# Two attention heads side by side in TensorE's array, slots placed anew, and a third of the pooling on ScalarE

## The reference

```python
# x: (64, 12, 224, 224); channel_weights (12, 192)
pooled = x.reshape(B, 12, 14, 16, 14, 16).sum(axis=(3, 5))       # patches of 16 x 16
h = einsum('bcij,ce->bije', pooled, channel_weights)             # 196 tokens of 192
h = h + attention1(layernorm(h))                                 # one head, Wq, Wk, Wv
x = layernorm(h)
# router: softmax over 4 experts; each expert takes its top 98 of 196 tokens
# expert e sees the first 24, 48, 96 or 192 channels; h1 = xg @ w1.T + b1, summed over experts
x_mlp, x_qkv = h1[..., :768], h1[..., 768:]
attn = softmax(q @ k.T * 16 ** -0.5)                             # 12 heads of 16, 196 x 196
y2 = concat(gelu(x_mlp), attn @ v)
o = (gathered y2 @ w2.T + b2) * mask, weighted by the gate, halves added
out = h + (x + o)
```

## Time and profile before

| | |
|---|---|
| median of 3 runs | 1757.34 us (1749.19 to 1767.99) |
| profiled execution | 1757.22 us, span 1755.4 us |
| mean granted clock of TensorE | 0.939 |
| busy: PE, DVE, ACT, POOL | 1517.8, 1218.5, 847.3, 248.9 us |
| mean DMA rate | 124 GB/s |

### The profile page before, as it was taken

One profiled execution on the slowest core, in us unless ns is written; L12 is line 12 of the kernel. 1 busy time (PEld: TensorE's weight loads), 2 busy tenths in 40 slices (PEclk: granted clock), 3 DMA queues, 4 the chain that ended last, 5 costly groups with the idle time before them and its releaser, 6 DMA issues.

```text
span 1755.4 us, 34644 instructions
## 1 busy us (share of the span) xinstructions
PE 1517.8 (86%) x12440; PEld 1258.9 (72%) x12440; DVE 1218.5 (69%) x2824; ACT 847.3 (48%) x1934; POOL 248.9 (14%) x319
## 2 busy tenths in 40 slices
PE   2146889898998999988998899989899989999998
PEld 2033778687786878777786777778687778878786
DVE  6658678757887578766887488765787677563552
ACT  0002555455554465454554555545554555546653
POOL 3021012200211002200111002300022002110000
PEclk9986889889999899998999899999899999989999
DMA  8985665516662475615673366706655152102220
GB/s 228 241 205 159 164 159 149 144 42 159 170 184 60 110 180 150 163 34 144 162 181 95 86 161 171 187 15 158 145 151 145 38 147 51 35 19 60 50 53 15
DMA packets 99574, 218.02 MB, mean 124 GB/s; under 512 B 61359, under 2 KB 75853, under 8 KB 88654
## 3 DMA queue, kind: packets, MB, share of 16 engines
q10 hardware_dynamic: 12032, 150.94, 32.4%
q1 hardware_dynamic: 87374, 64.88, 16.4%
HBM read 186.57 MB, written 28.90 MB: 123 GB/s over the span
## 4 chain that ended last, share of the span: by engine, by line
PE 50%; DVE 24%; issue 13%; DMA 7%; POOL 3%; ACT 2%; SPq 0%; DVEq 0%; POOLq 0%; ACTq 0%
PE bank L1050 12%; DVE psums L1258 9%; DVE peaks L1458 6%; PE bank L955 6%; PE bank L1019 5%; PE bank L985 5%; PE bank L1004 4%; DMA xt<-in_x_dram 4%; DMA qs<-shiftT 3%; PE bank L967 3%; POOL var L1590 2%; PE bank L878 2%; PE bank L1028 2%; PE bank L829 2%; PE bank L942 2%
## 5 line engine op out<-in xcount | busy, mean ns | idle before, releaser
L1458 DVE TENSOR_REDUCE peaks<-bank 98x2 f32<-98x392 f32 x768 | 423.3, 563 | 173.4 <-PE bank L985 152.7
L1207 ACT ACTIVATE Pb<-bank 98x392 f32<-98x392 f32 x768 | 374.5, 497 | 301.8 <-PE bank L1004 253.3
L1258 DVE TENSOR_REDUCE psums<-xt 112x2 f32<-112x512 f32 x672 | 425.8, 677 | 39.0 <-DMA xt<-in_x_dram 20.8
L1050 PE MATMUL bank<-w2T,hid 128*98 128x192 f32 x1536 | 312.1, 343 | 0.0
L985 PE MATMUL bank<-ks,qs 96*98 96x196 f16 x1536 | 269.3, 262 | 41.8 <-DVE peaks L1458 37.3
L1004 PE MATMUL bank<-qs,ks 97*98 97x196 f16 x1536 | 269.0, 259 | 23.3 <-DMA qs<-shiftT 21.5
L985 PEld LDWEIGHTS bank<-ks,qs 96*98 96x98 f16 x1536 | 166.1, 128 | 132.0 <-DVE peaks L1458 65.2
L1050 PEld LDWEIGHTS bank<-w2T,hid 128*98 128x98 f32 x1536 | 249.9, 176 | 3.6
L1004 PEld LDWEIGHTS bank<-qs,ks 97*98 97x98 f16 x1536 | 167.7, 130 | 35.4 <-DMA qs<-shiftT 24.4
L1019 PE MATMUL bank<-Pb,vals 98*32 98x196 f32 x3072 | 172.6, 343 | 1.2 <-ACT Pb L1207 1.2
L1618 POOL TENSOR_TENSOR fin<-fin,both 98x384 f32<-98x384 f32 x64 | 63.9, 998 | 728.8 <-DVE fin L1483 728.8
(11 more groups left out here) (185 smaller groups left out, 1777.9 us busy)
## 6 DMA issues: line engine op xcount, KB each, us to landing
xt<-in_x_dram ACTq DMA_DIRECT2D x94, 1568.0 KB, 9.0
qk_scratch<-qk SPq DMA_DIRECT2D x64, 294.0 KB, 4.1
qs<-qk_scratch SPq DMA_DIRECT2D x192, 73.5 KB, 3.0
ks<-qk_scratch SPq DMA_DIRECT2D x192, 73.5 KB, 3.1
out_dram<-fin SPq DMA_DIRECT2D x64, 147.0 KB
xt<-in_x_dram SPq DMA_DIRECT2D x2, 1568.0 KB, 15.3
qs<-shiftT SPq DMA_DIRECT2D x128, 2.3 KB
hid<-in_L_ffn_w_dram SPq DMA_DIRECT2D x1, 1440.0 KB
```

The costliest lines, as they stand in the source:

```text
L1050: mm = pe.matmul(misc_ps[slot][0:HT, D * h:D * h + D], lhs, w2T[0:w, f, :], start=(f == 0), stop=(f == NF + 1))
L1207: act.activation(Pb[:, (H * i + h) % NP, :, :].rearrange("p a b -> p (a b)"), score_ps[s][0:HT, 0:2 * T], ACT.Exp, scale=float(DH) ** -0.5 ...
L1258: last = dve.tensor_reduce(psums[:, m % 2, t, 2 * p:2 * p + 2], v[:, 2 * p:2 * p + 2, :, :], AX.XY, ALU.add)
L1458: dve.tensor_reduce(peaks[:, h // 6, :, h % 6], peak_ps[s][0:HT, 0:2 * T].rearrange("p (q k) -> p q k", q=2), AX.X, ALU.max, negate=True). ...
```

## The change

1. `KS` becomes 48. Even heads stand at partitions 0 to 48 and odd heads at 64 to 112 (`ODD`), each with its own row for the shift. `peak` and `score` do nothing for odd `h`; for even `h` they multiply both heads, alternating between the two halves, into two banks that are now one tile of two banks. VectorE's maximum and ScalarE's exponential cover both heads in one instruction, with one semaphore for each. `stack` issues eight DMAs instead of six, and `shift` two instead of one for each part. The columns of `M` are ordered accordingly, with one more copy, and the large memsets of `qs` and `ks` are gone.
2. From the last pair of images of group 1 on, the middle tile of each three (`SPLIT`) is pooled by ScalarE: 14 activations (`window`), one for each patch column, that copy 256 elements into the scratch tile `spent` and add them into `psums` by the accumulator output. VectorE has 14 instead of 21 pieces for two images. Before that point VectorE pools as it did.
3. The placing: `FC2_SLOTS`, `TAKE` 22, wider distances in `routing`, `choosing` one slot later, a floor of 0.65 for the credit of the choice's rounds, `planes` later behind the last piece and for one pair in the next section, pooling ahead of the slot's peaks in the later slots, new costs in the tables.

```diff
-KS = 96
+KS = 3 * DH
+ODD = 64
+FC2_SLOTS = (0, 3, 6, 7, 8, 9)
...
-def pooling(dg, m, at, more=True, turn=1.2, behind=3.5):
+def pooling(dg, m, at, more=True, turn=1.2, behind=3, split=False):
...
+        if split and t == SPLIT:
+            first, until = at[PIECES] + 0.5, at[2 * PIECES - 1] + 0.4
+            for j in range(GRID):
+                slot = first + (until - first) * j / GRID
+                ops.append((slot, ("window", dg, m, t, j)))
+        else:
+            for p in range(PIECES):
+                slot = at[PIECES * (t - (split and t > SPLIT)) + p]
+                ops.append((slot, ("pool", dg, m, t, p)))
+        row = max(slot + 1, row + 0.1)
+        ops.append((row, ("own_row", dg, m, t)))
...
-        credit = min(credit + cost(TENSOR, plan[at]) - cost(VECTOR, plan[at]), 2)
+        credit = min(credit + max(cost(TENSOR, plan[at]) - cost(VECTOR, plan[at]), 0.65), 2)
...
-    ops += [(at, ("gate_scale", dg)), (at + 2, ("gate_logits", dg)), (at + 5, ("gates", dg)),
+    ops += [(at, ("gate_scale", dg)), (at + 2 + wide / 2, ("gate_logits", dg)), (at + 5 + wide, ("gates", dg)),
...
-TAKE = 25
+TAKE = 22
+SPLIT = 1
-VECTOR = {"peak": 0.52, "choose": 1.05, "first_max": 0.52, "take": 0.9, "norm1_scale": 0.9, "norm1": 0.8, "shift1": 1,
+VECTOR = {"peak": 0.45, "choose": 1.05, "first_max": 0.52, "take": 0.9, "norm1_scale": 0.9, "norm1": 0.8, "shift1": 1,
-TENSOR = {"peak": 0.35, "score": 0.35, "mix": 0.65, "fc2": 0.89, "hidden": 2, "project": 1.33, "values": 0.66,
+TENSOR = {"peak": 0.19, "score": 0.19, "mix": 0.65, "fc2": 0.89, "hidden": 2, "project": 1.33, "values": 0.66,
...
-                fill[4 + k] = [("fc2", 0, i - 1, k)] + fill[4 + k]
+                fill[FC2_SLOTS[k]] = [("fc2", 0, i - 1, k)] + fill[FC2_SLOTS[k]]
...
-    front, at = routing(1, TAKE)
+    front, at = routing(1, TAKE, 2)
...
-    for slot, op in in_slots(choosing(1, at + 1) + turning(1, at + 4)):
+    began = int(at)
+    at = rounds(plan, 1, began)
+    quiet = (began, at + 4)
+    for slot, op in in_slots(choosing(1, at + 2) + turning(1, at + 4.5)):
         plan[slot].append(op)
-    pieces = TILES * PIECES
+    pieces = (TILES - 1) * PIECES
...
-    front = []
+    front = [(2, ("planes", 1, AHEAD - 1)), (4, ("tok", 1, AHEAD - 1))]
...
+        into = plan[min(slot, len(plan) - 1)]
+        peaks_at = [k for k, other in enumerate(into) if other[0] == "peak"]
+        into.insert(peaks_at[0] if slot >= H * GRP and peaks_at else len(into), op)
...
             def peak(at, G_, dg, i, h):
 
-                s = h % 2
+                if h % 2:
+                    return
                 if h == 0:
-                    pe.wait_ge(stack_in[i % NSTACK], 96 * (len(range(i % NSTACK, GRP, NSTACK)) * G_ + i // NSTACK + 1))
-                pe.wait_ge(peak_free[s], 6 * (GRP * G_ + i) + h // 2 + ONE)
+                    pe.wait_ge(stack_in[i % NSTACK], 128 * (len(range(i % NSTACK, GRP, NSTACK)) * G_ + i // NSTACK + 1))
+                pe.wait_ge(peak_free, 6 * (GRP * G_ + i) + h // 2 + ONE)
                 for q in range(2):
-                    mm = pe.matmul(peak_ps[s][0:HT, T * q:T * q + T],
-                                   qs[0:KS, i % NSTACK, h, HT * q:HT * q + HT], ks[0:KS, i % NSTACK, h, :],
-                                   start=True, stop=True)
-                mm.then_inc(peak_full[s], 1)
+                    for s in range(2):
+                        mm = pe.matmul(peak_ps[0:HT, s, T * q:T * q + T],
+                                       qs[ODD * s:ODD * s + KS, i % NSTACK, h // 2, HT * q:HT * q + HT],
+                                       ks[ODD * s:ODD * s + KS, i % NSTACK, h // 2, :], start=True, stop=True)
+                        if q == 1:
+                            mm.then_inc(peak_full, 1)
...
+            def window(at, G_, dg, m, t, j):
+
+                n_ = TILES * m + t
+                if j == 0:
+                    act.wait_ge(x_in[n_ % NX], 16 * (TILES * (GRP // PAIR) // NX * G_ + n_ // NX + 1))
+                    act.wait_ge(masked, 4 * G_ + max(m - 1, 0))
+                    act.wait_ge(pooled_act, done_by(True, G_, n_) - 1)
+                v = xt[:, n_ % NX, :].rearrange("p (k j w) -> p j k w", k=PATCH, w=PATCH)
+                last = act.activation(spent[:, j, :, :], v[:, j, :, :], ACT.Identity,
+                                      accum_out=psums[:, m % 2, t, j:j + 1])
+                if j == GRID - 1:
+                    last.then_inc(pooled_act, 1)
...
-                act.activation(Pb[:, (H * i + h) % NP, :, :].rearrange("p a b -> p (a b)"), score_ps[s][0:HT, 0:2 * T],
-                               ACT.Exp, scale=float(DH) ** -0.5).then_inc(score_free[s], 1)
+                at_ = (H * i + h) % NP
+                act.wait_ge(score_full, H * n_ + h + 2)
+                act.activation(Pb[:, at_:at_ + 2, :, :].rearrange("p s a b -> p s (a b)"), score_ps[0:HT, :, 0:2 * T],
+                               ACT.Exp, scale=float(DH) ** -0.5).then_inc(score_free, 1)
...
-                dve.tensor_reduce(peaks[:, h // 6, :, h % 6],
-                                  peak_ps[s][0:HT, 0:2 * T].rearrange("p (q k) -> p q k", q=2),
-                                  AX.X, ALU.max, negate=True).then_inc(peak_free[s], 1)
+                dve.wait_ge(peak_full, 2 * n_)
+                dve.tensor_reduce(peaks[:, h // 6, :, :, h % 6 // 2].rearrange("p q s -> p s q"),
+                                  peak_ps[0:HT, :, 0:2 * T].rearrange("p s (q k) -> p s q k", q=2),
+                                  AX.X, ALU.max, negate=True).then_inc(peak_free, 1)
```

More of the change, by code:

```diff
@@ L239, in prologue @@
     plan = [in_order(front + turning(0, at + 0.5 * ROUNDS + 3))] + opening(0, False)
-    for slot, op in in_slots(pooling(1, 2, steadily(1, 0.24))):
-        plan[min(slot, len(plan) - 1)].append(op)
+    for slot, op in in_slots(pooling(1, AHEAD - 1, steadily(1, 0.24))):
+        if op[0] not in ("planes", "tok"):
+            plan[min(slot, len(plan) - 1)].append(op)
     return sum(plan, [])
@@ L345, in body @@
         for m in range(AHEAD):
-            front += pooling(2, m, at[pieces * m:])
+            front += pooling(2, m, at[pieces * m:], behind=5, split=True)
     for slot, op in in_slots(front):
-        plan[min(slot, len(plan) - 1)].append(op)
+        if op[0] in ("planes", "tok") and op[1:] == (2, AHEAD - 1):
+            continue
+        into = plan[min(slot, len(plan) - 1)]
+        peaks_at = [k for k, other in enumerate(into) if other[0] == "peak"]
+        into.insert(peaks_at[0] if slot >= H * GRP and peaks_at else len(into), op)
     return sum(plan, [])
@@ L494, in bass_vit_tower @@
         w2T = sb("w2T", [128, NF + 2, D])
-        banks = [ctx.enter_context(nc.psum_tensor(f"bank{b}", [128, 512], F32)) for b in range(8)]
-        score_ps = banks[0:2]
-        peak_ps = banks[2:4]
-        misc_ps = banks[4:8]
+        score_ps, peak_ps = (ctx.enter_context(nc.psum_tensor(f"{n_}_ps", [128, 2, 512], F32)) for n_ in ("score", "peak"))
+        misc_ps = [ctx.enter_context(nc.psum_tensor(f"misc{b}", [128, 512], F32)) for b in range(MISC)]
+        banks = [score_ps[:, 0, :], score_ps[:, 1, :], peak_ps[:, 0, :], peak_ps[:, 1, :]]
         qk_dram = nc.dram_tensor("qk_scratch", (2, 2, 2, 2, DH, H // 2 * T), F16, kind="Internal").ap()
@@ L635, in x_tile, with windowed, done_by, wait_pooled @@
             return x.rearrange("b c (i k) w -> (b c i) (k w)", k=PATCH)[bass.ds(first_plane * GRID, PP), :]
+        def windowed(G_, n_):
+            return n_ % TILES == SPLIT and (G_ > 1 or (G_ == 1 and n_ >= TILES * AHEAD))
+        def done_by(act_too, G_, n_):
+            per = TILES * GRP // PAIR
+            return sum(windowed(*divmod(k, per)) == act_too for k in range(per * G_ + n_ + 1))
+        def wait_pooled(eng, G_, n_):
+            if windowed(G_, n_):
+                eng.wait_ge(pooled_act, done_by(True, G_, n_))
+            else:
+                eng.wait_ge(pooled, done_by(False, G_, n_))
         def settled(eng):
@@ L1193, in project @@
                     act.wait_ge(misc_full[slot], k + 1)
-                    act.copy(qk16[:, m, 0, :, :].rearrange("p c t -> p (c t)"), misc_ps[slot][0:DC, 0:2 * T]) \
+                    act.copy(qk16[:, :, 1 + m, :], misc_ps[slot][0:DC, 0:2 * T].rearrange("p (c t) -> p c t", c=2)) \
                         .then_inc(hi_ready, 1)
@@ L1489, in fc2 @@
                     dve.sem_inc(free, 1)
-            dve.memset(qs[:, :, :, :], 0.0)
             dve.memset(vals[:, :, :, :, :], 1.0)
```

127 lines of the change are left out of this document (64 added, 63 removed).

## The result

The changed kernel takes 1839.24 us (median of 4 runs, 1832.4 to 1841.88), the kernel before 1761.93 beside it (4 runs): a ratio of 1.044, 95% interval 1.037 to 1.051. The profiled execution has a span of 1840.1 us and a mean granted clock of 0.890; before had 1755.4 and 0.939. The forecast was 1667 with a range up to 1740.

The account below looks back on a forecast made before the run. TensorE was taken to bound the group's end and nearly its middle, where others stop it. Matmuls -26, waits -52, clock -10 and the last section's waits -2 sum to -90 us, giving about 1667 us, range 1585 to 1740.

Parts of the forecast that it names:

- A visit: TensorE switching to another array shape and back: about 0.30 us when float32 follows, read from the columns of `mix`.
- -26: TensorE's attention matmuls: us saved net by overlapping heads after paying for shape switches, with bounds of -131 and +105.
- the waits: TensorE's waits on other engines and transfers: -7.4 us a group, -52 us in seven, with bounds of 0 and -105.
- +0.5: The shift's row: us added where it is waited for, since SyncE issues two DMAs one behind the other.
- The 1.9 I took off: TensorE's wait for a bank that VectorE hasn't read: from 2.4 to 0.5 us, as fewer pooling pieces stand ahead.
- the clock: TensorE's granted clock: shorter gaps give some back, 1.5 us a group, -10 us in seven, bounds 0 and -20.
- the 0.96 that I started from: TensorE's clock in the repeated part, as a share of 2.4 GHz: some 8% of the time at 1.2 GHz.
- ScalarE's queue takes the gain: Rival: pooling copies among ScalarE's exponentials put 2.5 of each tile's 8.4 us onto the path, +62, 1729 us; chance 0.20.
- No overlap: Rival: the two heads' matmuls on TensorE don't overlap, 131 us of saving is lost, 1798 us; chance 0.06.
- two slots later, 2 us or more: VectorE's peaks: when the next pair is written, against 0.97 us to reduce one; 3.2 of 4.7 us waits taken off.

Follow-up runs that it names:

- e_heads_only: Part 1 of the change alone, on the kernel before, with its placing and all pooling on VectorE: 1781.24 us, ratio 1.0105.
- e_pair_full: The kernel before with two heads to one wait, one reduction and one exponential, each matmul still on the full array: 1783.98 us, ratio 1.0164.
- e_peaks_48: e_pair_full with its peaks multiplied over 48 rows instead of 96, so in the half shape: 1864.86 us, ratio 1.0596 to the kernel before.
- e_one_half: The changed kernel with both heads of a pair on the lower half of the array, so they can't overlap: 1901.83 us, ratio 1.079 to the kernel before.
- e_places_fc2: The changed plan with heads apart, all pooling on VectorE and `fc2` in its old slots: 1745.63 us, ratio 0.9942 to the kernel before.
- e_apart_fc2: e_places_fc2 with the pooling of ScalarE added, its copies written over the tile itself: 1793.86 us, ratio 1.0196 to the kernel before.
- e_fetch_joined: e_places_fc2 with the fetch of each middle tile held until that of the last of three: 1803.17 us, ratio 1.0229 to the kernel before.

## Why the prediction was wrong

**What held.** The heads overlap as columns do: the two matmuls of a pair start 3 ns apart, four of `peak` take 0.21 us where I had 0.17. The page TensorE: Matmul & The Clock Gate (Part 3) of the Trainium skill has about 4 ns for that, and the trace agrees. A visit costs 94 ns on entry, 89 on exit and 79 for the second float32 matmul behind it (medians in e_heads_only, at full clock), 0.26 us where I had read 0.30 from `mix`. The drain of which the TensorEngine Tiling page of the Trainium skill (Key Properties) speaks is thus there for rows too: the trace agrees, with these 94 and 89 ns. The stream shrank by 15.1 us a group, where 131 in eight groups is 16.4. Reductions (0.973 for 0.97) and exponentials (0.821 for 0.85) came as forecast. So "-26" for TensorE's matmuls held in kind, and fell short of the gain: 15.1 - 7.3 = 7.8 a group, where it had about 3.3.

**The step that failed most: "the waits", -8.9 + 1.5 = -7.4 a group.** They rose by 8.9. I had the shift's row at +0.5, for a second DMA to issue. It measured +4.5 (3.3 to 7.8 a group), and two reasons are shown by the runs. `fc2`'s new slots took one of two parts of `fc2` from between the shift's transpose in slot 2 and the first score that reads the row, in slot 6: with all pooling on VectorE the wait from 420 to 1220 us goes from 4.6 to 21.1 by these slots alone. And pooling on ScalarE doubles up the fetches: with the old slots it takes the same wait from 4.6 to 28.1. For the transfer's time isn't that of its issue but of what is in flight with it: 6 us for two pieces of 1.1 KB at 671.46. In the earlier trace rows it stood at 6.4 and 6.6 us for 2.3 KB; I used these rows for the length of a group only. The waits for `chosen` and the planes, 2.9 and 2.1 a group, did go, as I had them, and the peaks' fell by 0.4 instead of 3.2; but new ones came, for exponentials (2.0), `both` (1.7), `on_tok` (1.6) and `first_exp` (1.2), all of them results that VectorE or ScalarE hand to TensorE and that were in time before. The 1.9 I took off for the bank VectorE hasn't read became +1.9:

```profile
827.07 0.86 ACT L1249 CAST qk<-misc 96x392 f16<-96x392 f32 x2 [4.20 <-DMA qk_scratch<-qk]
...
828.25 1.68 PE L990 MATMUL misc<-UT,M 104*128 104x196 f32 x4 [4.36 <-DVEq L1509]
```

ScalarE's half of the next `project` waits for q and k to leave for DRAM, a DMA again, VectorE's half waits for ScalarE's, and TensorE for the bank. VectorE had the time that I gave it and could do nothing with it.

**The second: "the clock", -10 us with bounds of 0 and -20.** It cost 9.9 us a group, some 70 in all. I had tied it to long gaps alone. The page TensorE: Matmul & The Clock Gate of the Trainium skill (Part 1) says that idleness throttles and activity releases; the trace agrees only in part, since the stretch from 648.5 to 665.6 has 0.5 us of gaps and stays at 1.2 GHz throughout. Also, the 0.96 that I started from is that of one stretch; over the four groups the clock before was 0.94. Two things go with a lower clock here: the half shape (13.3 to 19.1 a group from e_pair_full to e_heads_only, to 20.0 in e_peaks_48, to 22.9 in e_one_half), and longer waits (7.8 to 14.1 from e_places_fc2 to e_apart_fc2), though e_fetch_joined, with as much waiting, has only 10.1. The first wasn't among my rivals. Why the clock is lower over such matmuls stays open: the runs show that it is, that bare visits hardly do it, and that it is as low without the overlap.

**The rivals.** "ScalarE's queue takes the gain" had the right place and the wrong mechanism: pooling on ScalarE costs 25 us in the changed kernel and 9 to 48 in the others, though its tile takes 5.6 us and not 8.4, and though TensorE waits for exponentials only 2.0 us a group. "No overlap" is refuted. The sum in the prediction's own terms, per group: stream -15.1 (forecast -16.4), switches +7.3 (+13.1), waits +8.9 (-7.4), clock +9.9 (-1.4).

**Pairs aren't free either.** Bundling two heads in one wait, which I costed only in VectorE's time, costs about 24 us in e_pair_full: TensorE's waits for peaks go from 4.9 to 8.0 us a group, which fits a pair of banks that must be read in full before the next may begin. I had written that the next comes "two slots later, 2 us or more". In the changed kernel the wait for peaks is 4.5, and the other waits are longer.

## What to carry to other kernels

Half-height matmuls side by side halve their stream, but count the switches (0.26 us a visit beside float32 work) and then take the clock from a run, not from the gaps: of 15 us a group gained, the switches took 7 in the changed kernel, and the clock took 6 in e_heads_only against e_pair_full. Before work is moved off an engine, look for short DMAs that TensorE waits for, and at what large transfers are in flight then: moving every third fetch by a few slots cost 57 us with no arithmetic changed. A wait is to be sized by the whole time of its transfer in the trace of before, with the cover that the edit takes away.

## What the hardware showed that I had not expected

- The granted clock is 0.93 with the attention's products on the full array (e_pair_full) and 0.88 to 0.90 with all or half of them on half of it (420 to 1220 us), at nearly the same waits in sum.
- A 73.5 KB transfer took 14.6 us with two 1568 KB tiles in flight, against 3.1 by the median. The shift's row of 2.3 KB took 1.7 us with none in flight, 4.4 with one and 9.3 with two (medians of before; the last is a single row).
- A copy of 256 elements with an accumulator starts every 0.40 us on ScalarE (674.27 to 674.67): the read of the sum, 0.19 us from 674.58, overlaps the next copy.
